# Two convolution parts moved into attention steps, and the next image's group statistics taken from a second read in 512-column blocks

## The reference

```python
x = x + _L0_conv_ref(_gn(x), Wqkv, bqkv, Wout, bout)     # 8-head attention over the 1024 pixels
x = x + _L1_conv_ref(_gn(x), ...)                        # deformable attention in 16 windows of 8 x 8
```

## Time and profile before

| | us |
|---|---|
| runs shown (3) | 3265.95 to 3269.01, median 3268.49 |
| profiled execution | 3270.41 |
| its span in the trace | 3268.6 |
| TensorE busy | 3007.1 |
| VectorE busy | 2188.8 |
| ScalarE busy | 1689.8 |
| GpSimd busy | 283.4 |

### The profile page before, as it was taken

The page is one execution under the profiler, slowest core; times in us unless marked ns, Lnnn a source line. Parts: engine busy times, 40 slices in busy tenths (PEclk is TensorE's granted clock), DMA queues, the critical chain, the costliest instruction groups (busy, mean ns, idle before and its releaser), DMA issues.

```text
span 3268.6 us, 51509 instructions
## 1 busy us (share of the span) xinstructions
PE 3007.1 (92%) x20600; PEld 2109.6 (65%) x20600; DVE 2188.8 (67%) x2902; ACT 1689.8 (52%) x2461; POOL 283.4 (9%) x189
## 2 busy tenths in 40 slices
PE   6999699998999989999999989999899998997857
PEld 5777577756766567665777557775677756775434
DVE  5666566686676866767667766667667686665855
ACT  2553455375553655536554555536455365553625
POOL 0000020001200020001200012000120001200121
PEclk9999899999999999999999999999999999998958
DMA  5223012311124011341013211232112311104030
GB/s 186 56 56 109 15 33 82 116 49 49 35 75 158 5 49 35 79 155 39 21 41 131 88 40 29 61 117 74 41 35 82 125 38 49 35 11 160 20 93 26
DMA packets 141502, 220.58 MB, mean 67 GB/s; under 512 B 77713, under 2 KB 96660, under 8 KB 137396
## 3 DMA queue, kind: packets, MB, share of 16 engines
q1 hardware_dynamic: 136596, 190.03, 18.4%
q10 hardware_dynamic: 4672, 27.26, 2.7%
HBM read 162.40 MB, written 54.84 MB: 66 GB/s over the span
## 4 chain that ended last, share of the span: by engine, by line
PE 72%; DVE 13%; issue 6%; ACT 4%; DMA 3%; SPq 1%; POOL 0%; POOLq 0%; DVEq 0%; ACTq 0%
PE banks L668 14%; PE banks L683 13%; PE banks L652 12%; PE banks L623 7%; PE banks L613 5%; PE banks L723 4%; PE banks L858 4%; PE banks L868 3%; PE banks L859 3%; PE banks L860 3%; DVE exps L1490 2%; PE banks L831 2%; DMA point_outputs_dram<-point_outputs 2%; ACT exps L1075 2%; DVE qk_halves L1586 2%
## 5 line engine op out<-in xcount | busy, mean ns | idle before, releaser
L1408 DVE TENSOR_REDUCE neg_max<-banks 128x1 f32<-128x1024 f32 x512 | 601.5, 1215 | 103.3 <-PE banks L652 102.2
L1417 DVE COPY exps_turned<-banks 128x1024 f32<-128x1024 f32 x256 | 313.3, 1224 | 492.8 <-PE banks L668 488.9
L1085 ACT ACTIVATE exps_turned<-banks 128x1024 f32<-128x1024 f32 x256 | 262.4, 1025 | 718.4 <-PE banks L668 718.4
L1075 ACT ACTIVATE exps<-banks,neg_max 128x1024 f32<-128x1024 f32 x512 | 564.9, 1112 | 67.6 <-DVE neg_max L1408 66.5
L668 PE MATMUL banks<-ident,exps 128*128 128x128 f32 x4096 | 557.6, 280 | 16.0 <-DVE exps_turned L1417 15.1
L668 PEld LDWEIGHTS banks<-ident,exps 128*128 128x128 f32 x4096 | 453.6, 142 | 174.3 <-issue 133.6
L652 PE MATMUL banks<-qk_halves 64*128 64x512 f32 x3072 | 444.6, 422 | 97.2 <-ACT exps L1075 59.7
L683 PE MATMUL banks<-exps_turned,values 128*64 128x256 f32 x4096 | 479.4, 383 | 0.8 <-issue 0.8
L652 PEld LDWEIGHTS banks<-qk_halves 64*128 64x128 f32 x3072 | 291.3, 192 | 184.1 <-issue 144.5
L683 PEld LDWEIGHTS banks<-exps_turned,values 128*64 128x64 f32 x4096 | 279.7, 137 | 153.6 <-issue 30.5
L1586 DVE SCALAR_TENSOR_TENSOR qk_halves<-banks,qk_halves 128x1024 fp32r<-128x1024 f32 x256 | 301.6, 1217 | 88.6 <-ACT qk_halves L1124 88.4
(11 more groups left out here) (182 smaller groups left out, 3440.7 us busy)
## 6 DMA issues: line engine op xcount, KB each, us to landing
wqk_ring<-wqk_split SPq DMA_DIRECT2D x62, 512.0 KB, 4.0
wo_halves<-wo_split_dram SPq DMA_DIRECT2D x8, 2048.0 KB, 7.7
exps_turned<-in_x SPq DMA_DIRECT2D x32, 512.0 KB, 5.3
x_dram<-exps SPq DMA_DIRECT2D x32, 512.0 KB, 2.6
exps_turned<-x_dram SPq DMA_DIRECT2D x32, 512.0 KB, 6.2
out<-exps_turned SPq DMA_DIRECT2D x32, 512.0 KB, 2.6
recips_b<-recips_dram SPq DMA_DIRECT2D x240, 64.0 KB, 3.5
x_image<-in_x ACTq DMA_DIRECT2D x14, 1024.0 KB, 13.6
```

The costliest lines, as they stand in the source:

```text
L1075: freed(act.activation(PB[:, 2 * h + n % 2], slot(("s", m, i)), ACT.Exp, bias=NM[:, m:m + 1], accum_out=SS[:, m:m + 1]), ("s", m, i))
L1408: dve.tensor_reduce(NM[:, m:m + 1], slot(("s", m, i)), AX.X, ALU.max, negate=True).then_inc(mx, 1)
L1417: dve.tensor_copy(PT[:, n // 2 % 2, 1, :, P * j:P * j + P], TB.rearrange("p s (k q) -> p (s k) q", k=4)).then_inc(t_free[1], 1)
```

## The change

The four convolution parts are split. The parts 0 and 1 stay in the tail. The products of parts 2 and 3 go to VectorE's steps 0 and 2 of the next image and their sums to steps 1 and 3, each ahead of the step's copy. For the last image they follow the tail. `PROD` moves out of the exponentials' tile into that of the attended values. The gelu, tanh and log on ScalarE go to steps 3, 4 and 5, the offsets' matmuls to step 4 (into the other PSUM bank), and VectorE's small operations to steps 5 to 13, now ahead of the copies.

The group statistics of the next image no longer come from the image in its tile. SP issues eight extra loads per image of 128 channels by 512 columns, 256 KB each, into two tiles in turn (`CVS` and `SMB`, shared with the convolution sums and the probabilities), two behind each `recips_around(u)` for u = 5 to 8. VectorE takes the statistics of block c in step 12 + c, ahead of that step's copy; the means follow in step 20, the group sums in step 22. The image itself is still loaded in step 22; it is normalised in steps 25 and 26, and `x_low` has steps 27 to 30. `rows_to_dram` goes from u = 5 to u = 6.

The last addition changes hands: `result` on VectorE adds product, bias and residual in one instruction from PSUM and replaces `keep_result` and `add_residual`; two run between the low halves of queries and keys, two behind the first maxima. GpSimd's affine of the pixels waits for the 28th maximum of the next image where it waited for the 16th.

```diff
         RR = OT_ALL.bitcast(BF16)
-        PROD = PB[:, 0:2].rearrange("p a n -> p (a n)")[:, 0:1600]
+        PROD = OT_ALL[:, 2048:3648]
...
         RB = sb("recips_b", [P, 2, 256])
-        T4 = sb("conv_sums", [P, 256])
-        TG = sb("conv_gelu", [P, CT, 64])
+        CVS = sb("conv_or_sample", [P, 512])
+        T4 = CVS[:, 0:256]
...
         SM = sb("sim", [P, PXT * CT, 8])
-        SMP = sb("probabilities", [P, 2, 4, 32])
-        AT2 = sb("probabilities_turned", [P, 4, 64])
+        SMB = sb("probs_or_sample", [P, 512])
+        SMP = SMB[:, 0:256].rearrange("p (h l e) -> p h l e", h=2, l=4)
+        AT2 = SMB[:, 256:512].rearrange("p (c n) -> p c n", c=4)
+        XSAMPLE = (CVS, SMB)
...
 
+            def load_sample(c, k):
+                wait_after(sp, xs_done, 8 * (k - 1) + c - 1)
+                if c < 2:
+                    wait_after(sp, o1_full, 2 * (k - 2))
+                sp.dma_start(XSAMPLE[c % 2][:], x[k, P * (c // 2):P * (c // 2) + P, 512 * (c % 2):512 * (c % 2) + 512])\
+                    .then_inc(xs_in[c % 2], 16)
+
             for i in range(B):
                 for u in range(OUTS - 1):
                     recips_around(u, i)
-                    if u == 5 and i:
+                    if i + 1 < B and 5 <= u < 9:
+                        load_sample(2 * u - 10, i + 1)
+                        load_sample(2 * u - 9, i + 1)
+                    if u == 6 and i:
...
                 rstd(LRS[:], LVE[:], PXT, ln_var, ln_rstd, i + 1)
-                if i:
-                    add_residual(i - 1)
                 if i + 1 < B:
-                    pool.wait_ge(mx, (i + 1) * TILES + 16)
+                    pool.wait_ge(mx, (i + 1) * TILES + 28)
                 wait_full(pool, ("tc", CT - 1, i))
                 for r in range(PXT):
...
                 wait_after(pe, piece_free, (i * 3 + p - 1) * PIECES + which)
+                if n == 6 and i:
+                    pe.wait_ge(off_done, i)
                 project_halves(MB, WQ[:, w], c, range(CT)).then_inc(piece_full, 1)
...
                     if i and n == 26:
                         sampled_keys(i - 1)
-                    if i + 1 < B and n == 26:
-                        group_sums(2 * i + 2, GSO)
+                    if i + 1 < B and n == 22:
+                        pe.wait_ge(piece_free, (i + 1) * MAXES)
+                        group_sums(2 * i + 2, GSM)
                     if i and n == 27:
...
 
+            def sample_stats(c, k):
+                dve.wait_ge(xs_in[c % 2], 64 * (k - 1) + 16 * (c // 2 + 1))
+                dve.bn_stats(BNS[:, c // 2, c % 2], XSAMPLE[c % 2][:]).then_inc(xs_done, 1)
+
             def group_channels(last):
                 link(last)
+                channel_means()
...
 
-            def convolve(n, i):
+            def convolve_mult(n):
                 oy, ox = n // 2, n % 2
                 q = A[:].rearrange("p t (u y x) -> p (t u) y x", y=8, x=8)[:, :, 3 * oy:3 * oy + 5, 3 * ox:3 * ox + 5]
                 w = CW[:].rearrange("p (y x) -> p y x", y=6)[:, 1 - oy:6 - oy, 1 - ox:6 - ox]
                 prod = PROD.rearrange("p (u y x) -> p u y x", y=5, x=5)
-                if n == 0:
-                    dve.wait_ge(x2_out, 64 * (i + 1))
-                link(dve.tensor_tensor(prod, q, w.unsqueeze(1).broadcast_to([P, 64, 5, 5]), ALU.mult))
-                ins = dve.tensor_reduce(T4[:].rearrange("p (u o) -> p u o", o=4)[:, :, n],
+                return mark(dve.tensor_tensor(prod, q, w.unsqueeze(1).broadcast_to([P, 64, 5, 5]), ALU.mult))
+
+            def convolve_sum(n, after):
+                dve.wait_ge(dve_step, after)
+                ins = dve.tensor_reduce(T4.rearrange("p (u o) -> p u o", o=4)[:, :, n],
...
+            def result(t, j):
+                dve.wait_ge(o1_full, 2 * j + t // 2 + 1)
+                dve.wait_ge(xr_in[t], x2_loads(j))
+                y = XR[:, t].rearrange("p (r n) -> p r n", r=4)
+                dve.scalar_tensor_tensor(out=y, in0=ROWS_OUT[:, t % 2], scalar=BO1[:, t:t + 1], in1=y, op0=ALU.add,
+                                         op1=ALU.add).then_inc(y_done, 1)
 
...
                     if i + 1 < B:
-                        if n == 24:
+                        if 12 <= n < 20:
+                            sample_stats(n - 12, i + 1)
+                        if n == 20:
+                            dve.wait_ge(xs_done, 8 * (i + 1))
+                            channel_means()
+                        if n == 25:
                             dve.wait_ge(x_in[0], 16 * (i + 1))
-                            group_parts(X, 0)
-                            group_parts(X, 1)
-                        if n == 25:
-                            dve.wait_ge(x_in[1], 16 * (i + 1))
-                            group_parts(X, 2)
-                        if n == 26:
-                            group_channels(group_parts(X, 3))
-                        if n == 27:
                             dve.wait_ge(gn_rstd, 2 * i + 2)
                             normalise(0)
                             normalise(1)
-                        if n == 28:
+                        if n == 26:
+                            dve.wait_ge(x_in[1], 16 * (i + 1))
                             normalise(2)
                             normalise(3)
-                        if n == 29:
-                            x_low(1, i + 1)
-                        if n == 30:
...
+                        if 27 <= n < 31:
+                            x_low(n - 27, i + 1)
                     if n % 2:
                         if n < STEPS - 1:
                             recips(n // 2, i)
                         if n >= 5:
                             outputs(n // 2 - 2, i)
+                    if i and n in (0, 2):
+                        multiplied = convolve_mult(n // 2 + 2)
+                    if i and n in (1, 3):
+                        convolve_sum(n // 2 + 2, multiplied)
+                    if i and n == 5:
+                        sample_points(i - 1)
+                        log_inputs(i - 1)
+                    if i and n == 6:
+                        hats(i - 1)
+                    if i and n == 7:
+                        log_split(i - 1)
+                    if i and 8 <= n < 14:
+                        log_row((n - 8) // 2, (n - 8) % 2, i - 1)
                     copy_turned(n, i)
-                    if i + 1 < B and n == 26:
-                        group_variance(2 * i + 2, GSO)
+                    if i + 1 < B and n == 22:
+                        group_variance(2 * i + 2, GSM)
                     if i and n == 26:
...
                         key_blocks(i - 1)
-                    if i + 1 < B and n == 29:
-                        x_low(2, i + 1)
...
-                    if i and n == 2:
-                        sample_points(i - 1)
-                    if i and n == 3:
-                        log_inputs(i - 1)
-                    if i and n == 4:
-                        hats(i - 1)
-                    if i and n == 5:
-                        log_split(i - 1)
-                    if i and 6 <= n < 12:
-                        log_row((n - 6) // 2, (n - 6) % 2, i - 1)
...
                     wait_emptied(dve, ("lq", t, i))
-                for n in range(4):
-                    if n == 2 and i and i + 1 < B:
-                        low("q", 0, 0, i + 1, q_hi)
-                    convolve(n, i)
+                for n in range(2):
+                    convolve_sum(n, convolve_mult(n))
+                if i and i + 1 < B:
+                    low("q", 0, 0, i + 1, q_hi)
+                for t in range(2 if i else 0):
+                    result(t, i - 1)
                 if i + 1 < B:
                     if i:
                         low("k", 2, 4, i + 1, k_hi)
                     for h in range(2):
                         row_max(h, i + 1)
+                for t in range(2, CT if i else 0):
+                    result(t, i - 1)
+            for n in range(2, 4):
+                convolve_sum(n, convolve_mult(n))
             sample_points(B - 1)
             log_inputs(B - 1)
             hats(B - 1)
...
             bias_softmax(B - 1)
+            for t in range(CT):
+                result(t, B - 1)
```

62 lines of the change are left out of this document (21 added, 41 removed).

## The result

The changed kernel takes 3336.12 us (median of 4 runs, 3334.77 to 3339.76) against 3268.75 before: a ratio of 1.0202, 95% interval 1.0179 to 1.0226. The forecast was 3338. The profiled execution took 3339.76 with a span of 3337.9, 69.3 longer than before.

A forecast was written before the change was run, and what follows sets the result against it. TensorE, busy 92% of the span, was taken to bound the kernel. Profiled 3270.4 us plus 138.5 of stall cost minus 69 won gave 3340, against the median 3338; range 3285 to 3395.

The forecast's parts named there:

- The stall's mechanism and place: Steps 12, 14, 16, 18: sample loads behind SP's 8.51 us wait land after VectorE needs them; copies 18.2 us apart.
- Its size: Stall of 18.5 us per image, 129.5 over seven, plus 9 for the clock: 138.5 us; block landing taken as 3.1.
- The first block: Step 12: the first sample block makes VectorE's copy 4.4 us late; the three later even blocks lose 4.7 each.
- the 1.3 charged to the clock: After the last wait, one group of TensorE's scores at lowered clock: 1.3 us per image, 9 in all.
- GpSimd beside the statistics, taken at 0: Steps 12 to 16: GpSimd's affine might lengthen bn_stats by 0 to 25 us in all; 0 was taken.
- Tails: Between images: TensorE's 4.84 us wait for keys' low half shrinks; 33 us won in images 1 to 6, 7.4 in image 0.
- Steps 2 and 6: The two long pairs of steps lose most of their 1.24 us excess each: 1.6 us won per image, 11 in all.
- Steps 24 to 30: Statistics leave these steps: 2.1 us won, less 0.5 for the group sum in step 22; 1.6 per image, 11 in all.
- End: After the last image: last adds move from GpSimd to VectorE, and the chain of small operations shortens; 7 us won.
- The rivals without a stall or with half of one: Steps 12 to 18: blocks in time, 3199 us, chance 0.06; or write returns sooner and landing 2.5, 3268 us, chance 0.08.
- The rival of the queue in the tail: Tail: VectorE's four results and the keys queue up, TensorE waits as long as now; 3371 us, chance 0.11.
- the slow landing: Sample loads: each block takes 5.3 us to land, beside other queues or GpSimd; 3400 us, chance 0.10.

The follow-up runs named there:

- loads_first: The change with the two sample loads of a round issued ahead of the write of the reciprocals on SP's queue; 3196.12 us, 0.9770 of the kernel before.
- stats_later: The change with VectorE's statistics of block c taken in step 13 + c, one step later, and the means in step 21; 3201.42 us, ratio 0.9801.
- round_short: The change with reciprocals written as 128 pieces of 16 bytes, not 512 of 4; output not the reference's; 3188.69 us, 0.9748 of the kernel before.
- loads_ahead: The change with the sample loads issued right behind the write of the reciprocals, ahead of SP's wait for it; 3268.66 us, 1.0007 of the kernel before.
- conv_in_tail: The change without its second read, and with all four convolution parts back in the tail; 3271.29 us, 0.9996 of the kernel before.

## Why the prediction was right

*The stall's mechanism and place:* right. The circle in the chain above is the one written down, and its period was forecast as 18.2; the three pairs took 18.64, 18.75 and 18.26 on average over seven images. loads_first, stats_later and round_short each remove the stall, or nearly, in a different way. Each even block waited 6.2 us where 4 were named as the sign. What the prediction didn't see is why the round is slow: it counted the wait as a delay of SP's alone, and by that loads_ahead should have cured it. On the forecast this had no bearing, since the change puts the loads behind the wait.

*Its size:* 152.6 against 138.5. The landing was 3.8 us, not 3.1 (inside the bounds of 2.5 and 5.3), nor the 2.6 of the other estimate in the prediction; in the circle a shorter round made up for most of it, 1703.56 to 1716.88 being 13.3 us against 13.15. The first block was mis-sized too: 5.4 us late instead of 4.4. On average over the seven images it landed 3.9 us after its issue (3.1 were counted), and the copy started 1.2 us after the statistics (0.7), while SP's round was 0.3 shorter than counted. In image 4, where the copy came 0.83 behind, a log row's copy stands between the two:

```profile
1698.55 0.69 DVE L1353 BATCH_NORM_STATS2 bn_stats<-conv_or_sample 128x6 f32<-128x512 f32 x1 [7.96 <-DMA conv_or_sample<-in_x]
1699.16 0.29 DVE L1539 COPY attended<-log_parts 64x512 bf16<-64x512 bf16 x1
1699.38 1.21 DVE L1418 COPY exps_turned<-banks 128x1024 f32<-128x1024 f32 x1
```

The rest of the 0.5 us by which the copy came later isn't placed. The three pairs lost 15.2 us instead of 14.1. The last pair took 14.64 against 13.49, 1.1 us for the 1.3 charged to the clock. That the 8 us by which TensorE's work took longer at 0.88 lie inside the waits fits these sums, but no run shows it by itself.

*GpSimd beside the statistics, taken at 0:* right. Their durations stayed at 0.67 to 0.70 us, and loads_first, with GpSimd's 20 us in the same steps, has about 1 us more per image there than before; three of its eight blocks in image 4 ran beside GpSimd, in 0.67 to 0.68 us.

*Tails:* 32.7 + 8.2 against 33 + 7.4. The keys' low half and the 4.84 us went as described, in each of images 1 to 6; the single tails, which hold much else, gave 2.9 to 6.6. With the results on VectorE the gain hangs on the split (conv_in_tail); the split with ScalarE and GpSimd still adding was not run.

*Steps 2 and 6:* 1.74 us per image against 1.6; in image 4 the pair with step 2 gave 1.24, that with steps 5 and 6 0.70, and the next lost 0.20. *Steps 24 to 30:* 48.3 against 48.5 in image 4. All of steps 20 to 31 gave 17.7 where 11 were forecast. In five of images 1 to 6 it is 2.7 us each for the 1.6 counted: 2.25 between the copies of steps 23 and 30, 2.0 of it in step 24, where the first statistics stood (2.1 were counted), and 0.4 in step 31; the group sum charged with 0.5 cost nothing that shows, as the copies of steps 20 to 23 lie as far apart as before. Image 2 gave 4.2, image 0 only 0.5. *End:* 11.5 against 7, another mis-sized term: the adds are gone (two results, 2.48 us), and the rest is the last image's chain; the gain at the end varies from 11 to 17 us between the kernels that share it, so its split is not settled.

So the mechanism was right, but that the sum hit 69 to a few tenths was luck: two errors cancel, a cost 14 too low and gains 14 too low. The rivals without a stall or with half of one needed a round under the 10 us that the earlier trace rows showed; the rows were right. The rival of the queue in the tail fell with the 0.68 us, the slow landing with 3.8 us against 5.3.

## What to carry to other kernels

A load issued behind a wait in a queue is as late as that wait, and what counts is its landing against the first instruction that asks, on an in-order engine with the next stage's input behind it. Ahead of the wait is not enough: put it ahead of the slow transfer. And look at the shape of a small DMA: for the same 2 KB SP waited 1.55 us in pieces of 16 bytes, 3.1 in pieces of 8 and 8.5 in pieces of 4.

## What the runs showed of the hardware that was not expected

A write of single 4-byte numbers to DRAM shows its packets at once and ends late. DMA activity in after from 1684.6 to 1692.5, while SP waits for one (40 equal slices, tenths of the 16 engines' time, GB/s):

```profile
DMA  0018300000000000000000000000000000000000
GB/s 0 0 1 7 3 0 0 0 0 0 0 0 0 0 0 0 0 0 0 0 0 0 0 0 0 0 0 0 0 0 0 0 0 0 0 0 0 0 0 0
DMA packets 528, 0.00 MB, mean 0 GB/s; under 512 B 528, under 2 KB 528, under 8 KB 528
```

All 528 packets (512 numbers and 16 more) pass in three slices, 0.6 us; then the trace shows nothing moving for some 7 us until the wait ends. A load issued behind it, in loads_ahead from 1660.7 to 1670.4:

```profile
DMA  8116972100000022090653350470255802002006
GB/s 7 1 51 228 388 279 76 51 8 0 0 0 0 0 17 17 8 93 17 34 25 17 17 17 8 8 17 8 17 8 8 25 17 8 0 8 8 8 17 68
```

Some 264 KB of the two blocks' 512 move in the first nine slices of 0.24 us, at up to 388 GB/s; after that the rate is mostly 8 to 34 GB/s, until SP's wait ends at 1669.0 and the first block lands at 1670.3. With pieces of 4 bytes the wait is 8.5 us for 512 and 7.7 for 256, with 256 of 8 bytes 3.1, with 128 of 16 bytes 1.55. So it isn't the count alone. Whether it is the size of a piece, or how many pieces fall side by side in DRAM, isn't told apart here, and why a load's last packets come so slowly while such a write is open wasn't tried.
